# x of a state-space kernel turned to token rows by DVE 32x32 block transposes and sixteen SBUF-to-SBUF transfers per chunk, in place of eight TensorE transposes

## The reference

```python
xBC = silu(conv(proj) + conv_b)            # hs (x), Bm, Cm
scores   = einsum('bcihn,bcjhn->bcijh', Cc, Bc) * Ldec * dtc[:, :, None]
y_intra  = einsum('bcijh,bcjhp->bcihp', scores, xc)
states   = einsum('bcjh,bcjhn,bcjhp->bchpn', dtc * dlast, Bc, xc)
y_inter  = einsum('bcihn,bchpn->bcihp', Cc * exp(cum), prev)   # prev: scanned states
y = y_intra + y_inter + D * x
g = y * silu(gate);  g = rms_norm_per_group(g) * norm_w;  out = g @ out_w.T
```

## Time and profile before

| | |
|---|---|
| median of the runs | 1737.63 us |
| profiled execution, first to last instruction | 1737.2 us |
| PE busy | 1724.5 us (99%), weight load 1436.9 (83%) |
| DVE, ACT, POOL busy | 1221.0, 1192.8, 1182.1 us (70, 69, 68%) |
| DMA packets' time, share of 16 engines | 42% |
| granted TensorE clock, mean | 0.999 |

### The profile page before, as it was taken

One profiled execution on the slowest core, in us unless ns is written; L12 is line 12 of the kernel. 1 busy time (PEld: TensorE's weight loads), 2 busy tenths in 40 slices (PEclk: granted clock), 3 DMA queues, 4 the chain that ended last, 5 costly groups with the idle time before them and its releaser, 6 DMA issues.

```text
span 1737.2 us, 27735 instructions
## 1 busy us (share of the span) xinstructions
PE 1724.5 (99%) x9925; PEld 1436.9 (83%) x9925; DVE 1221.0 (70%) x2154; ACT 1192.8 (69%) x2232; POOL 1182.1 (68%) x1058
## 2 busy tenths in 40 slices
PE   9999999999999999999999999999999999999999
PEld 7788888888888888888888888888888888787887
DVE  8886778768785769676875878586867688663323
ACT  6887677767867677767776777768777777663421
POOL 5586768677777668676867687766867686774510
PEclk9999999999999999999999999999999999999999
DMA  5534435343543443443534354345343353444201
GB/s 192 171 107 116 125 116 169 109 119 105 162 128 114 121 146 112 121 116 112 174 115 115 97 162 128 114 122 151 114 118 113 110 174 101 118 114 134 80 15 49
DMA packets 122056, 211.63 MB, mean 122 GB/s; under 512 B 24256, under 2 KB 28992, under 8 KB 121920
## 3 DMA queue, kind: packets, MB, share of 16 engines
q1 hardware_dynamic: 121920, 209.87, 41.7%
HBM read 205.09 MB, written 4.72 MB: 121 GB/s over the span
## 4 chain that ended last, share of the span: by engine, by line
PE 97%; DVE 1%; DMA 1%; POOL 0%; ACT 0%; issue 0%; POOLq 0%
PE bank L1712 19%; PE bank L1714 18%; PE bank L1713 18%; PE bank L1788 7%; PE bank L1846 7%; PE bank L1836 7%; PE bank L1829 7%; PE bank L1803 5%; PE bank L1762 2%; PE bank L2091 1%; PE bank L2092 1%; PE bank L2093 1%; PE bank L1862 1%; PE bank L1772 1%; PE bank L1953 1%; DMA w_raw<-in_wp 0%
## 5 line engine op out<-in xcount | busy, mean ns | idle before, releaser
L704 POOL TENSOR_TENSOR w_l<-w_raw,w_h 128x512 fp32r<-128x512 f32 x288 | 379.6, 1321 | 341.2 <-ACT w_h L900 341.2
L1712 PE MATMUL bank<-x_h,w_h 128*128 128x512 f32 (+1 forms) x1328 | 527.0, 397 | 3.9 <-DVE x_ch L1385 2.3
L1714 PE MATMUL bank<-x_h,w_l 128*128 128x512 f32 (+1 forms) x1328 | 519.7, 391 | 0.0
L1713 PE MATMUL bank<-x_l,w_h 128*128 128x512 f32 (+1 forms) x1328 | 518.1, 390 | 0.0
L1385 DVE SCALAR_TENSOR_TENSOR x_ch<-bank,par,x_ch 128x511 f32<-128x511 f32 (+2 forms) x384 | 287.2, 749 | 80.3 <-ACT x_ch L918 71.2
L953 ACT ACTIVATE decay<-decay,cols 128x128 f32<-128x128 f32 x1024 | 318.2, 390 | 3.7 <-DMA cdec<-cdec_scratch 1.6
L1712 PEld LDWEIGHTS bank<-x_h,w_h 128*128 128x128 f32 (+1 forms) x1328 | 249.5, 188 | 55.1 <-issue 3.1
L1714 PEld LDWEIGHTS bank<-x_h,w_l 128*128 128x128 f32 (+1 forms) x1328 | 249.2, 188 | 54.6
L1713 PEld LDWEIGHTS bank<-x_l,w_h 128*128 128x128 f32 (+1 forms) x1328 | 249.7, 188 | 51.1
L1415 DVE TENSOR_TENSOR decay<-decay,bank 128x512 f32<-128x512 f32 x256 | 171.3, 683 | 107.1 <-ACT decay L953 107.1
L918 ACT ACTIVATE x_ch<-bank,par 128x512 f32<-128x512 f32 x128 | 99.0, 774 | 185.6 <-PE bank L1714 185.5
(11 more groups left out here) (161 smaller groups left out, 2760.0 us busy)
## 6 DMA issues: line engine op xcount, KB each, us to landing
w_raw<-in_wp SPq DMA_DIRECT2D x288, 256.0 KB, 3.0
decay<-cum_scratch SPq DMA_DIRECT2D x256, 256.0 KB, 4.1
ec<-ecum_scratch SPq DMA_DIRECT2D x96, 256.0 KB, 6.2
ow_raw<-in_ow SPq DMA_DIRECT2D x64, 256.0 KB, 4.8
w_raw<-in_w SPq DMA_DIRECT2D x48, 256.0 KB, 2.7
acc<-in_x SPq DMA_DIRECT2D x8, 256.0 KB, 4.5
out<-acc SPq DMA_DIRECT2D x8, 256.0 KB, 2.0
cols<-cols_scratch SPq DMA_DIRECT2D x16, 96.0 KB, 2.7
```

What stands on the lines that cost most here:

```text
L704: pool.tensor_tensor(w_l[:, s, :], w_raw[:, s, :], w_h[:, s, :].bitcast(F32), ALU.subtract).then_inc(wl_ready, 1)
L1712: pe.matmul(dst, wh, xh, start=(opens and k == 0), stop=False)
L1713: pe.matmul(dst, wh, xl, start=False, stop=False)
L1714: last = pe.matmul(dst, wl, xh, start=False, stop=(k == len(terms) - 1 and not more))
```

## The change

PE's `turn_x` goes away, and with it `tx_done` and `x_chr`. DVE gets a `turn_x` that transposes 32x32 blocks of `x_ch` (128 x 1024 elements, one instruction) into a new tile `x_sq`, which lies in the bytes of `gT_l`. SP gets a `move_x`: sixteen transfers, each of 32 partitions x 1 KB, from `x_sq` to `xw`, so that each block lands on its token rows. `scale_x` then reads `xw` from SBUF in place of the `xt` banks. Because of the shared bytes, `move_x` waits for `st_done` of the chunk, `gT_low` of chunk K waits until the x of chunk K + 1 has been fetched, and DVE's `turn_x` waits for `out_half` of the chunk before last.

```diff
+        x_sq = under("x_sq", [P, QUADS, CT, SQ])
+        gT_l = sc("gT_l", [P, CT, P], F32R)
 sync
+            def move_x(g, k):
+                K = g * CHUNKS + k
+                sp.wait_ge(x_turned, K + 1)
+                if some(n_state(g, k)):
+                    sp.wait_ge(st_done, n_state(g, k))
+                for i in range(QUADS):
+                    for j in range(QUADS):
+                        sp.dma_start(xw[j * SQ:(j + 1) * SQ, i * CT * SQ:(i + 1) * CT * SQ],
+                                     x_sq[i * SQ:(i + 1) * SQ, j, :, :].rearrange("p n t -> p (n t)")).then_inc(x_fetched, 16)
...
                             load_decay(gn, kn, q)
+                        if c < SC - 1:
+                            move_x(gn, kn)
                     if more and kn % SC > 0:
...
                     for i in tiles[2 if first else 1:-1]:
                         load_next_w(g, last, b, i)
+                    if c == SC - 1:
+                        move_x(gn, kn)
 gpsimd, gT_low
                 pool.wait_ge(gTh_ready, K + 1)
+                if not (isinstance(g, int) and K == GROUPS * CHUNKS - 1):
+                    pool.wait_ge(x_fetched, 16 * QUADS * QUADS * (K + 2))
 vector, scale_x
-                dve.wait_ge(tx_done, K + 1)
+                dve.wait_ge(x_fetched, 16 * QUADS * QUADS * (K + 1))
...
-                for h in range(2):
-                    last = dve.tensor_tensor(per_head(xdt[:, half(h)]), per_head(xt[h][:, :]),
-                                             spread(cols[:, b, DT, c, h * 8:h * 8 + 8], HDIM), ALU.mult)
+                for a in range(2):
+                    by = dts[:, a, :].unsqueeze(2).unsqueeze(3).broadcast_to([P, CT, QUADS // 2, SQ])
+                    last = dve.tensor_tensor(xd[:, a, :, :, :], xs[:, a, :, :, :], by, ALU.mult)
+            def turn_x(g, k):
+                K, b, c = g * CHUNKS + k, k // SC, k % SC
+                if c == 0:
+                    dve.wait_ge(silu_done, conv_no(2 * g + b, CONV_TILES))
+                if some(K) and some(K - 1):
+                    dve.wait_ge(out_done, 2 * (K - 1))
+                dve.transpose(x_sq.rearrange("p b n t -> p n b t"), x_ch[:, b, :, tok(c)]).then_inc(x_turned, 1)
...
                         fade(g, k)
+                    if c < SC - 1:
+                        turn_x(gn, kn)
                     add_skip(g, k)
+                    if c == SC - 1:
+                        turn_x(gn, kn)
 tensor
-            def turn_x(g, k):
...
-                for n in range(CT):
-                    last = pe.transpose(xt_r[n // 4][:, tok(n % 4)], x_chr[:, b, n, tok(c)], ident_r[:, :])
-                last.then_inc(tx_done, 1)
...
                     if last and c == SC - 1:
                         match(gn, kn)
                         projects(tiles[1:-1])
-                        turn_x(gn, kn)
                     else:
-                        turn_x(gn, kn)
                         match(gn, kn)
```

More of the change, by code:

```diff
@@ L33 @@
 PIECE = KT * P
+SQ = 32
+QUADS = P // SQ
 SLOT_TILES = [[("g", 0), ("g", 1), ("c", 0), ("c", 1), ("g", 2)],
@@ L163, in build @@
         sgT_r = sc("sgT_r", [P, BATCH, CT, SEQ], F32R)
-        x_ch = under("x_ch", [P, BATCH, CT, SEQ])
-        x_chr = sc("x_chr", [P, BATCH, CT, SEQ], F32R)
+        x_ch = sc("x_ch", [P, BATCH, CT, SEQ])
         ow_h = sc("ow_h", [P, CT, HID], F32R)
@@ L182, in build @@
         y_r = sc("y_r", [P, CT, P], F32R)
-        gT_h, gT_l = sc("gT_h", [P, CT, P], F32R), sc("gT_l", [P, CT, P], F32R)
+        gT_h = sc("gT_h", [P, CT, P], F32R)
+        x_sq = under("x_sq", [P, QUADS, CT, SQ])
+        gT_l = sc("gT_l", [P, CT, P], F32R)
         b_tok_h, b_tok_l = sc("b_tok_h", [P, P], F32R), sc("b_tok_l", [P, P], F32R)
@@ L255, in build @@
         bank = [ctx.enter_context(nc.psum_tensor(f"bank{i}", [P, 512], F32)) for i in range(8)]
-        xt_r = [b.bitcast(F32R) for b in bank[2:4]]
         pj, xt, yb, cbb, ob = bank[0:2], bank[2:4], bank[4:6], bank[6], bank[7]
@@ L324, in build @@
         early_gates = sem("early_gates")
-        tx_done = sem("tx_done")
+        x_turned = sem("x_turned")
+        x_fetched = sem("x_fetched")
         mt_done = sem("mt_done")
@@ L570, in _ @@
                 sp.wait_ge(cols_stored[n], 32 if n < 2 else 16)
+            move_x(0, 0)
             sp.wait_ge(rows_stored, 16 * BATCH)
@@ L601, in last_chunk @@
                         load_decay(LAST, k + 1, q)
+                    move_x(LAST, k + 1)
                     sp.wait_ge(z_scaled, n_across(LAST, k + 1))
@@ L1513, in _ @@
                     copy_cols(1)
+            turn_x(0, 0)
             ow_low(0, OW_EARLY)
@@ L1566, in last_chunk @@
                 if k == SC:
+                    turn_x(LAST, k + 1)
                     add_skip(LAST, k)
@@ L1580, in last_chunk @@
                 gate_up(pairs[0] - 1)
+                if k < CHUNKS - 1:
+                    turn_x(LAST, k + 1)
                 fade(LAST, k)
@@ L1720, in norm_transpose @@
                     pe.wait_ge(x_l_ready, c - 3)
-                if k == 1 and c in (2, SC, SC + 1):
-                    pe.wait_ge(xdt_ready, (GROUPS - 1) * CHUNKS + (SC if c == 2 else c + 2) + 1)
+                if k == 1 and c == 2:
+                    pe.wait_ge(x_l_ready, CHUNKS + 1)
+                if k == 1 and c in (SC, SC + 1):
+                    pe.wait_ge(state_ready, n_state(GROUPS - 1, c + 2))
                 if k == 1 and c == SC - 1:
@@ L1750, in project @@
                                                 for q in range(KT)]).then_inc(pj_done, 1)
-            def turn_x(g, k):
-                K, b, c = g * CHUNKS + k, k // SC, k % SC
-                if c == 0:
-                    pe.wait_ge(silu_done, conv_no(2 * g + b, CONV_TILES))
-                if K == MIDDLE + 1:
-                    pe.wait_ge(x_l_ready, CHUNKS + 2)
-                if some(K):
-                    pe.wait_ge(xdt_ready, K)
-                    pe.wait_ge(state_ready, n_state(g, k))
-                for n in range(CT):
-                    last = pe.transpose(xt_r[n // 4][:, tok(n % 4)], x_chr[:, b, n, tok(c)], ident_r[:, :])
-                last.then_inc(tx_done, 1)
             def match(g, k):
@@ L1813, in new_state @@
                 pe.wait_ge(xw_l_ready, n_state(g, k) + 1)
-                pe.wait_ge(xdt_ready, K + 1)
+                if some(n_state(g, k)):
+                    pe.wait_ge(state_ready, n_state(g, k))
                 if g == GROUPS - 1 and k in (SC, CHUNKS - 2):
@@ L1860, in square_total @@
                 if K == MIDDLE:
-                    pe.wait_ge(xdt_ready, K + 2)
+                    pe.wait_ge(x_l_ready, CHUNKS + 2)
                 pe.matmul(total_of(K), y[:, 0, :], ones[:, :], start=True, stop=True).then_inc(ss_done, 1)
@@ L1913, in _ @@
             project(0, 1, 0)
-            pe.wait_ge(cols_out, KINDS * BATCH)
-            turn_x(0, 0)
             LAST = GROUPS - 1
@@ L1967, in last_chunk @@
                     project(LAST, 1, TILES - 1)
-                    turn_x(LAST, k + 1)
                     match(LAST, k + 1)
```

3 lines of the change are left out of this document (added).

## The result

| | before | after |
|---|---|---|
| median of the runs | 1737.97 us (1737.61 to 1738.37, 4 runs) | 2360.85 us (2359.16 to 2362.37, 4 runs) |
| ratio | | 1.358 (95% interval 1.356 to 1.3599) |
| profiled execution, first to last instruction | 1737.2 us | 2358.0 us |
| granted TensorE clock, mean | 0.999 | 0.886 |

The change costs 621 us of span where I forecast 277: the sign was right, the time lies far above the range of 1890 to 2100 us. The page of the kernel after: busy time, the granted clock in 40 slices, the chain by engine, three of the costliest groups (busy us and mean ns, then idle time ahead and what ended it), two DMA issues (KB, us to landing).

A forecast was written before the change was run, and what follows sets the result against it. PE, 97% of the chain, was taken as the bound; 151 + 5 + 48 + 40 + 26 + 7 = 277 us, net of the transposes' gain, on 1737.2 gave 2014, 2015 for the median; range 1890 to 2100 us.

The forecast's parts named there:

- `scale_x`: On DVE, reading two SBUF tensors beside POOL's `gT_low`: from 1.29 us to 1.3 to 2.6, taken as 2.3.
- k = 0: Eight c = 0 chunks where DVE has no slack: `accumulate` ends at 17.0, +6 us each (3.5 to 8), 48 in all.
- c = 3: Fourteen chunks, move behind the tile 16 refill: PE idles 9.8 us, then a clock dip; +10.8 us each, 151 in all.
- the issue: Serial DMA issues on SP's queue: 0.47 us each, sixteen 7.5 us, x there 9.1 us after SP is free.
- the clock: Granted PE clock falling after a wait: one dip priced at 1.6 us, in c = 3 chunks.
- the last sequence: k = 4 to 6 of g = 7: `out_half` stands behind more products, so 0 us.
- chunk 59: Last group's c = 3 chunk, no refill ahead of the move, only `gT_low` late: +5 us, an estimate.
- c = 1: Fifteen chunks: `accumulate` 1.8 us late for PE, DVE's delay partly absorbed by waits; +2.7 us each (0.6 to 5), 40 in all.
- c = 2: With c = 0 at k = 4, 22 chunks where DVE has more waits to give: +1.2 us each (0 to 3), 26.
- Hidden: Rival: SP issues cost below 0.25 us each, so the move fits before the old `scale_x`; near 1700 us, chance 0.04.
- Mild: Rival: clock doesn't fall, `scale_x` stays near 1.3 us, the turn hides, c = 0 to 2 recover delay; 1903 us, chance 0.18.
- Heavy: Rival: late refills hold ACT 2 to 3 us more in 45 chunks, moved bytes slow `decay` loads; 2127 us, chance 0.16.

The follow-up runs named there:

- PE kept at work: Changed kernel plus unread filler products on PE ahead of the first `out_half` (20 with c < 3, 48 with c = 3), all chunks but the last five: 2280.02 us.
- with one transfer: Changed kernel with the sixteen transfers of a chunk made one of 128 rows x 4 KB, x left unsorted: 1897.3 us.
- the way through HBM: Changed kernel with x sent to HBM scratch in one transfer and back in four, ahead of c = 3's refills, `gT_low` waiting for the first alone: 1950.53 us.

## Why the prediction was wrong

**Right.** PE was the bound and its new waits were paid, but for k = 0, where DVE is the bound, as predicted. (PE's share of the chain fell to 47%, not to some 80.) The transposes give back 0.70 (0.63 predicted). The move of c = 3 starts at 8.7. A DVE turn takes 1.24 us (1.3), landing 1.8 (2.0). `accumulate` behind `scale_x` is what PE waits for; `gT_l` is next. The serial issues count and, outside k = 0, not the bytes.

**Wrong.** The terms that failed are the issue ("I take 0.47"; it was 0.63, times sixteen), `scale_x` ("I take 2.3"; it was 3.44) and the clock, priced for c = 3 alone. In the 59 chunks outside the last sequence and chunk 59 the issue makes 59 x 2.4 = 142 us, `scale_x` 59 x 1.1 = 65, and the clock 37 x 2.2 = 80. These are estimates worked out from the rows above and below; together 287 of the 344 us by which the loss is over the forecast.

*The clock in c < 3, and who is late there.* I took `accumulate` to be at 15.8 in c = 1, 1.8 late, and priced a dip of the clock for c = 3 alone, although the head had shown one after a wait of 2.27 us. With a wait of 5.3 `out_half` part 0 took 2.6 us longer in the c = 2 chunk shown; on the mean of the 37 chunks of its kind (c = 1, c = 2 and k = 4) the stretch behind the wait is 2.2 longer, 80 us in all. The run with PE kept at work gave 23.0 + 27.3 + 14.3 = 65 us back in these 37, although `out_half` started 0.24 us later in each (9 us), and nothing in k = 0, where DVE covers it. The size of the dip in c = 3 was nearly right (1.9 more from `out_half` to `inside` in the chunk shown, 2.2 in the mean one, 1.6 predicted).

*The issue.* 0.47 us was read from loads from HBM; an issue from SBUF to SBUF starts every 0.63. All 1024 of them:

```profile
L501 SPq DMA_DIRECT2D xw<-x_sq x1024: 507/591/1717, 80.2 to 2172.7; - x171
```

Sixteen last 10.05 us at the median and not 7.5 (10.0 to 11.4, mean 10.3), so that x is there 2.4 us later or more in every chunk. I had bounded landing and the turn from both sides, and not the issue, the term that is multiplied by sixteen: the rows that I took agreed so well with one another that I held the figure as fixed. A dearer issue stood in the trace of the kernel before, in a group that I hadn't read, the two loads of `ec` from HBM in each chunk with c > 0:

```profile
L487 SPq DMA_DIRECT2D ec<-ecum_scratch x96: 450/590/2272, 85.4 to 1548.5; - x96
```

Its median is that of the moved pieces, 0.59 us. So 0.6 us is not peculiar to a transfer from SBUF to SBUF, and a range up to it could have been read beforehand. The Trainium skill, "DMA: Bandwidth & Descriptors", section "SWDGE vs HWDGE vs iDMA", calls the time on the sequencer usually small relative to the DMA itself; here one issue takes 0.63 of the 1.8 us from issue to landing, and sixteen take 10.0, so the measurement decides against it, even more than I said.

*`scale_x`.* 3.44 and not 2.3. My row was four `ow_l` that stood beside `gT_low` for only part of the time; here both start within 0.12 us of each other, and the first half ends only when POOL's 2.77 us are over (its two halves take 2.83 and 0.69, and 1239.22 + 2.83 is 1242.05, where `gT_low` ends at 1242.11). +1.1 us in every chunk.
The Trainium skill, "SBUF — State Buffer", section "SBUF: two separate sides", has the rule that I left unused: a DVE operation with two SBUF inputs and a GpSimd one that reads SBUF share a pair of ports under an exclusive lock, and the one that comes second stands still for the whole of the other. By that rule this case's trace agrees on the full block; on who goes first it doesn't read so plainly, since `scale_x` has the earlier start by 0.12 us and is the one that waits.

Issue and `scale_x` make out 3.5 us of what the mean chunk with c = 2 is over the forecast (7.2 less 1.2 is 6.0), the clock 2.2; in the c = 3 chunk shown the two make 3.6 of 3.9 (31.7 less 27.9).

*k = 0.* `accumulate` ended at 20.4, not 17.0, and DVE's work from there to `inside` took 17.2 us, where it had been 15.2 (838.37 to 853.58). I had counted on some relief; `fade` went from 1.65 to 2.92 and the last two `ow_l` from 2.63 to 3.72, both with two sources in SBUF:

```profile
1174.64 4.82 DVE L1413 SCALAR_TENSOR_TENSOR ow_l<-ow_raw,par,ow_h 128x512 fp32r<-128x512 f32 x4
1179.39 2.92 DVE L1492 TENSOR_TENSOR state<-state,cdec 128x1024 f32<-128x1024 f32 x1
...
1185.65 3.72 DVE L1413 SCALAR_TENSOR_TENSOR ow_l<-ow_raw,par,ow_h 128x512 fp32r<-128x512 f32 x2
```

*The last sequence.* Priced at nothing because `out_half` stands behind more products. It does, and still PE waits there: 3.87 us for `gT_l` in the first of the three, 4.28 and 4.34 for `accumulate` in the others, and then four products take 2.05 us that take 1.07 at the upper level:

```profile
2141.76 2.05 PE L1878 MATMUL bank<-ow_h,gT_h 128*128 128x512 f32 x4 [4.28 <-DVE acc L1521]
```

In the three chunks together: +20 us. Chunk 59 lost 12.3 and not 5: PE waits 8.0 us for `gT_l` in its `out_half`, and the products behind it take 2.1 us per four.

*The rivals.* Hidden fell with the issue rate. Mild fell with the clock and `scale_x`. Heavy named late refills that hold ACT: ACT's waits for a raw weight did grow, from 4.4 us to

```profile
ACT w_h L922 <- DMA w_raw<-in_wp: 287.7, 39, 9.2
```

but the chunks with c = 2 add up without it, so I read this wait as covered; no run took it away by itself (with one transfer it went together with the issues), and the one with the move ahead of the refills in c = 3 made the chunks with c = 1, c = 2 and k = 4 longer by 0.25 us or less. The range failed because its ends were made of cases whose issue was 0.47 in all of them, and because three terms that all point the same way (issue, `scale_x`, clock) add 3.5 + 2.2 us in the 37 chunks of the kind above, and my range let them add up in one kind of chunk alone, c = 3.

**What stays open.** Why an issue of the moved pieces costs 0.6 us. Cutting them another way changed nothing, the `ec` loads from HBM cost as much, most other loads from HBM 0.33 to 0.43, the single large transfer from SBUF to SBUF 0.49, and in the way through HBM the issues took 0.43 each in both directions. Also open is why the clock fell behind some waits of 2.5 us and not behind others.

## What to carry to other kernels

A move that is cut into many transfers on one queue costs the number of its issues times an issue, so look through all kinds of issue in the trace and take the dearest as the upper end (here 0.59 us, where I took 0.47), before multiplying by sixteen. When PE sets the time, price a wait of some microseconds as the wait and the slower products behind it (5.4 and 2.2 us here, on the mean of 37 chunks), in each place where it occurs and not only in the worst. And when one semaphore releases two engines that both read SBUF, ask which of them is needed first and hold the other back.

## What the runs showed of the hardware

- A DMA issue on SP's queue: 0.46 us start to start for loads from HBM, but 0.59 long for the `ec` loads, also from HBM. From SBUF to SBUF 0.63 start to start, for 32 rows of 1 KB, and 0.64 for 128 rows of 256 B. 32 KB land 1.8 us after the issue, 512 KB in one transfer 4.0 at the median, and 7.8 to 9.0 in the k = 0 chunks, where other loads fill the DMA engines.
- A DVE instruction of 512 columns with both sources in SBUF took 0.69 us alone and 2.83 beside a POOL instruction of 2.77 that started 0.12 us after it: DVE got through when POOL was done. One of the same kind that reads PSUM took 0.68.
- DVE turned 128 x 1024 fp32 elements in 32x32 blocks in 1.24 us.
- The granted clock read 0.50 for 5.3 us behind a PE wait of 5.3 us, and 1.00 behind one of 1.18 with twenty products ahead of it. It made 2.7 us of `out_half` into 5.3. Behind 48 products and a wait of 2.5 us it read 0.50 in one chunk, and 1.00 behind a wait of 2.71 in another.
